# Graph network on one core: the dense pass writes no rows of its second norm, and the second attention's first pass normalises first-norm rows where a flag asks for it

## What is computed

```python
x = _layernorm(x + _L0_gnn_ref(x, src, dst, edge_weight, ...))     # GIN: two linear layers with batch norm
x = _layernorm(x + _L1_gnn_ref(x, edge_index, W, a))               # graph attention over src, 0 for nodes that are no src
x = _layernorm(x + _L2_gnn_ref(x, edge_attr_8, Wq, Wk, Wv, Wo, src, dst))   # attention over dst, 0 for nodes that are no dst
x = _layernorm(x + _L3_gnn_ref(x, edge_index, W, ...))             # graph attention with self loops
```

## Time and profile before

| | |
|---|---|
| median of 3 runs | 4597.76 us (4596.85 to 4601.44) |
| the profiled execution: time, span | 4595.28 us, 4593.2 us |
| busy share of the span | PE 76%, PE weight loads 57%, DVE 72%, ACT 56%, POOL 64% |
| mean granted TensorE clock | 0.853 |
| read from, written to DRAM | 351.68 MB, 389.16 MB |

### The profile page before, as it was taken

How to read it: one execution, slowest core, us unless ns; L and a number is a source line. 1 busy time by engine, 2 the same in 40 slices (tenths; PEclk the granted TensorE clock), 3 DMA queues, 4 the chain that set the end, 5 groups by cost and what they waited for, 6 DMA issues and landing times. The chain is left out here.

```text
span 4593.2 us, 91353 instructions
## 1 busy us (share of the span) xinstructions
PE 3488.3 (76%) x17524; PEld 2616.9 (57%) x17524; DVE 3319.8 (72%) x11837; ACT 2592.9 (56%) x6036; POOL 2942.8 (64%) x2825
## 2 busy tenths in 40 slices
PE   4899934446999997888888878777769958850587
PEld 2799922224888885555555645555558845530365
DVE  7788833334555567999999979888965577740798
ACT  0687712222666666777777748787854436640376
POOL 0366658885333335777777767888877836667476
PEclk9999955556999998998899877778889979985799
DMA  1688823333444447888888843333345537763344
GB/s 43 182 238 237 236 68 79 80 80 88 161 159 162 162 163 231 275 272 273 272 271 272 272 150 92 99 99 101 99 111 128 127 98 211 211 169 82 95 135 117
DMA packets 450182, 734.81 MB, mean 160 GB/s; under 512 B 171319, under 2 KB 284845, under 8 KB 450028
## 3 DMA queue, kind: packets, MB, share of 16 engines
q1 hardware_dynamic: 276204, 571.18, 40.5%
q0 software_dynamic: 173824, 162.17, 14.8%
HBM read 351.68 MB, written 389.16 MB: 161 GB/s over the span
## 5 line engine op out<-in xcount | busy, mean ns | idle before, releaser
L1222 PE MATMUL nodes_xp<-w_self,nodes_x3T 128*125 128x256 f32 x1600 | 493.6, 436 | 130.3 <-DVE nodes_elu L1333 123.5
L1080 POOL TENSOR_TENSOR mlp_r_parts<-mlp_r,mlp_r_parts 128x500 fp32r<-128x500 f32 x200 | 253.5, 1268 | 403.4 <-ACT mlp_r_parts L1066 394.2
L1371 POOL TENSOR_SCALAR nodes_x<-nodes_u,nodes_r,nodes_nm 125x256 f32<-125x256 f32 x800 | 459.8, 588 | 74.6 <-DVE nodes_nm L1326 67.8
L1222 PEld LDWEIGHTS nodes_xp<-w_self,nodes_x3T 128*125 128x125 f32 x1600 | 296.5, 206 | 208.7 <-issue 114.4
L774 PE MATMUL gram<-gin_both,gin_am 125*128 125x257 f32 x404 | 206.6, 667 | 266.2 <-DVE gin_both L757 254.0
L1379 POOL TENSOR_TENSOR nodes_v<-nodes_elu,nodes_x 125x512 f32<-125x512 f32 x200 | 253.7, 1269 | 176.6 <-DVE nodes_elu L1333 176.3
L1105 DVE BATCH_NORM_STATS2 mlp_stats<-mlp_y 128x500 f32 (+1 forms) x200 | 136.2, 681 | 255.6 <-ACT mlp_y L1056 255.6
L774 PEld LDWEIGHTS gram<-gin_both,gin_am 125*128 125x128 f32 x404 | 118.5, 323 | 354.2 <-issue 322.8
L178 POOL DMA_INDIRECT by_src<-rank_recs,rank_place x100 | 119.7, 1197 | 289.9 <-DVE rank_recs L504 289.3
L1019 PE MATMUL mlp_y<-mlp_hT,mlp_w 128*128 128x500 f32 x1200 | 296.7, 396 | 1.6 <-DVE mlp_hT L1099 0.9
L1019 PE MATMUL mlp_y<-mlp_r_parts,mlp_w 128*128 128x500 f32 x1200 | 287.4, 388 | 0.8 <-ACT mlp_y L1056 0.8
(11 more groups left out here) (406 smaller groups left out, 11561.4 us busy)
## 6 DMA issues: line engine op xcount, KB each, us to landing
X<-nodes_x SPq DMA_DIRECT2D x200, 448.0 KB
Y<-mlp_y SPq DMA_DIRECT2D x100, 500.0 KB
nodes_y<-Y SPq DMA_DIRECT2D x100, 500.0 KB
rank_xin<-x SPq DMA_DIRECT2D x100, 448.0 KB
XP<-rank_xc SPq DMA_DIRECT2D x100, 448.0 KB
mlp_h<-XP SPq DMA_DIRECT2D x100, 448.0 KB
nodes_x<-x SPq DMA_DIRECT2D x100, 448.0 KB
out<-nodes_out SPq DMA_DIRECT2D x100, 448.0 KB
```

Of the source, the lines that this page charges most:

```text
L1080: pool.tensor_tensor(rp[:, s, 1, m, :], r[:, s, m, :], rp[:, s, 0, m, :], ALU.subtract).then_inc(s_rp, 1)
L1222: pe.matmul(xp[:, b, j, :], x3T[:, s, k, P * j:P * j + P], w_self[:, k, 0:F], start=(k == 0), stop=False)
L1371: pool.tensor_scalar(dst[:, s, j, :], u[:, at.slot(LONG), j, :], r[:, s, k, j:j + 1], nm[:, s, k, j:j + 1], ALU.mult, ALU.add).then_inc(do ...
```

## The change

- The dense pass computes and stores no x2: two instead of three values of q, r and nm per row, two instead of four POOL instructions per tile at line 1371, no x2 store. SP loads a chunk's x ahead of its y, in place of y ahead of x.
- X1 and X2 become the two halves of one DRAM table XX of 2N rows; Y2 is laid over the second half, which the first attention then fills with the true x2 of every src node, by indices `write2`, computed on POOL ahead of its first gather.
- A dst that is no src has no x2 in the table. To know which, `histogram` adds SHIFT = 16384 to the table of places by dst wherever the count by src of the same node isn't zero. So these edges are scattered to a second region of the sorted list, both regions being cleared by two more DMAs beforehand, and `segments` loads both and adds them up. The fourth number of the record, now 1, comes out as the flag: 1 where the record lay in the second region.
- `attention_scores` gathers a dst row from dst + N * flag (`dst2`), a src row always from src + N. Each `xd` row goes through a layer norm, which for flag 1 has the variance replaced by 1 and the mean by 0. DVE does `stats`, `aggregate`, `variance`, ACT does `normed` (Ln, Exp, Copy, Identity), its result `xn` takes the place of `xd` in the transposes and the D2 store. `xs` gets 8 buffers. The lags and the order of the lists change as shown.

```diff
@@ histogram
+    by_dst = env["sorted"][1]
+    halves = [by_dst[a:a + E, :].rearrange("(p k u) r -> p k (u r)", p=P, k=10) for a in (0, SHIFT)]
...
+            for rows in halves:
+                sp.dma_start(rows, env["zcol"][0:P, 0:120].unsqueeze(1).broadcast_to([P, 10, 120])).then_inc(s_clear, 16)
...
+            ch.step(dve.tensor_scalar(incl[:, 0, :, :], count[:, 0, :, :], 1.0, float(SHIFT), ALU.min, ALU.mult))
+            ch.step(dve.tensor_tensor(base[:, 1, :, :], base[:, 1, :, :], incl[:, 0, :, :], ALU.add))
@@ segments
+            sp.dma_start(far[:, :, :], beyond).then_inc(s_dma, 16)
+            sp.dma_start(nxt_far[0:P - 1, :], beyond[1:P, 0, 0:2]).then_inc(s_dma, 16)
...
+            ch.step(dve.tensor_tensor(env["srec"][1][:, :, :], env["srec"][1][:, :, :], far[:, :, :], ALU.add))
+            ch.step(dve.tensor_tensor(nxt[:, 1, :], nxt[:, 1, :], nxt_far[:, :], ALU.add))
+            ch.step(dve.tensor_copy(env["srec"][1][:, :, 3], far[:, :, 3]))
@@ nodes
-                for k, (m, a) in enumerate(((1.0, EPS), (1.0 + EPS, EPS * EPS), (1.0 + EPS + EPS * EPS, EPS ** 3))):
+                for k, (m, a) in enumerate(((1.0, EPS), (1.0 + EPS + EPS * EPS, EPS ** 3))):
...
-                for k in range(3):
+                for k in range(2):
...
-                for k, (dst, done, stored) in enumerate(((x1, s_x1, o_1), (x2, s_x2, o_2))):
...
+                for j in range(J):
+                    pool.tensor_scalar(x1[:, s, j, :], u[:, at.slot(LONG), j, :], r[:, s, 0, j:j + 1], nm[:, s, 0, j:j + 1],
+                                       ALU.mult, ALU.add).then_inc(s_x1, 1)
@@ attention_scores
-                dram.gather(xd[:, s, :], env["X2"], meta["node"][:, at.col], s_d[s])
-                dram.gather(xs[:, s, :], env["X2"], meta["other"][:, at.col], s_s[s])
+                dram.gather(xd[:, s, :], env["XX"], dst2[:, at.col], s_d[s])
+                dram.gather(xs[:, l, :], env["XX"], src2[:, at.col], s_s[l])
...
+            def normed(at):
+                s = at.slot(RING)
+                act.wait_ge(s_q, at.count(2, 2))
+                ch = Chain(act, ca, at.count(3))
+                ch.step(act.activation(lnq[:, s, :], q[:, s, :], ACT.Ln, bias=rec[:, at.col, 3]))
+                ch.step(act.activation(c[:, s, :], lnq[:, s, :], ACT.Exp, scale=-0.5))
+                ch.step(act.activation(nm[:, s, :], mean[:, s, :], ACT.Copy, scale=c[:, s, :]))
+                wait(act, s_t, at.count(1, 1 - RING))
+                wait(act, s_o[s], at.uses(RING, 32))
+                act.activation(xn[:, s, :], xd[:, s, :], ACT.Identity, bias=nm[:, s, :], scale=c[:, s, :]).then_inc(s_xn[s], 1)
...
-            run_stages(act, [(0, copy_rows), (1, copy_out)], T)
+            run_stages(act, [(0, normed), (1, copy_rows), (3, copy_out)], T, **stages)
...
+            def variance(at):
+                s = at.slot(RING)
+                dve.wait_ge(s_mv, at.count(1, 1))
+                wait(dve, s_xn[s], at.uses(RING))
+                dve.scalar_tensor_tensor(out=q[:, s, :], in0=mv[:, s, 1:2], scalar=EPS, in1=fresh[:, at.col],
+                                         op0=ALU.add, op1=ALU.mult).then_inc(s_q, 1)
+                dve.tensor_scalar(mean[:, s, :], mv[:, s, 0:1], unfresh[:, at.col], None, ALU.mult).then_inc(s_q, 1)
...
-            run_stages(dve, [(0, rest), (1, dots)], T)
+            run_stages(dve, [(0, stats), (3, rest), (0, aggregate), (4, dots), (0, variance)], T, **stages)
```

More of the change, by code:

```diff
@@ L49 @@
 RC = 12
+SHIFT = 1 << 14
 CUTS = ((0, 112), (112, 13))
@@ L1379, in add @@
                 pool.tensor_tensor(v[:, s, :, :], el[:, s, :, :], x3[:, at.slot(LONG), :, :], ALU.add).then_inc(s_v, 1)
-            run_stages(pool, [(11, add), (6, first_two)], tiles, tiles, LONG, LONG)
+            run_stages(pool, [(11, add), (6, first)], tiles, tiles, LONG, LONG)
     ph.end()
@@ L1421, in _ @@
         def _(pool):
-            dram = Rows(ph, pool, N)
+            dram, second = Rows(ph, pool, N), Rows(ph, pool, 2 * N)
+            pool.tensor_scalar(write2[:, :], meta["write"][:, :], N, None, ALU.add).then_inc(s_index, 1)
+            pool.wait_ge(s_index, 1)
             def fetch(at):
@@ L1434, in put_x2 @@
                 pool.wait_ge(s_x2, at.count(1, 1))
-                dram.scatter(env["X2"], meta["write"][:, at.col], x2[:, s, :], s_w2[s])
+                second.scatter(env["XX"], write2[:, at.col], x2[:, s, :], s_w2[s])
             def put_xp(at):
@@ L1843, in attention_scores @@
     meta, rec = env["meta"][1], env["srec"][1]
-    xd, xs = ph.sb("xd", [P, RING, F]), ph.sb("xs", [P, RING, F])
+    LONG = 2 * RING
+    xd, xs, xn = ph.sb("xd", [P, RING, F]), ph.sb("xs", [P, LONG, F]), ph.sb("xn", [P, RING, F])
+    st, mv = ph.sb("stats", [P, RING, 6]), ph.sb("mv", [P, RING, 2])
+    q, mean, lnq, c, nm = (ph.sb(n, [P, RING, 1]) for n in ("q", "mean", "lnq", "c", "nm"))
+    fresh, unfresh = ph.sb("fresh", [P, T]), ph.sb("unfresh", [P, T])
+    dst2, src2 = ph.sb("dst2", [P, T], I32), ph.sb("src2", [P, T], I32)
+    s_index = ph.sem("index")
+    stages = dict(unroll=LONG, behind=LONG)
     xT = ph.sb("xT", [128, RING, 2, 4, P], F32R)
@@ L1902, in project @@
                 mm.then_inc(s_p, 1)
-            run_stages(pe, [(0, turn_rows), (1, project)], T)
+            run_stages(pe, [(0, turn_rows), (1, project)], T, **stages)
         @block.scalar
         def _(act):
+            def normed(at):
[8 more added lines that the diff above has]
+                act.activation(xn[:, s, :], xd[:, s, :], ACT.Identity, bias=nm[:, s, :], scale=c[:, s, :]).then_inc(s_xn[s], 1)
             def copy_rows(at):
```

128 lines of the change are left out of this document (73 added, 55 removed).

## The result

The changed kernel takes 4710.03 us (median of 4 runs, 4705.79 to 4713.15), the kernel before 4598.89 us on the same chip (4 runs, 4596.85 to 4601.44): ratio 1.0244, 95% interval 1.0228 to 1.0261. The prediction was 4695 us in a range of 4655 to 4745, slower. The profiled execution took 4713.15 us with a span of 4710.0 us, 116.8 more than the span before. DVE is busy for 71% of it, PE 74%, ACT 58%, POOL 58%; 352.28 MB were read and 339.16 MB written.

A forecast was written before the change was run, and what follows sets the result against it. DVE was taken to bound the dense pass, and a DVE-ACT loop the second attention's first pass, in place of POOL. -34 + 2 + 101 + 20 + 1 + 0.5 + 1 + 6 = +97.5 us on 4595.3; median 4695, range 4655 to 4745.

The forecast's parts named there:

- The loop over DVE and ACT: Second attention's first pass: DVE and ACT wait for each other every tile, 4.04 us against POOL's 3.03, +101 us.
- The clock: Second attention's first pass: PE at its low clock for a third of the tiles, 4.67 us each, +20 us.
- The dense pass: DVE's list gets 0.35 us shorter per pair of tiles, mostly through fewer POOL instructions: -34 us over 97 pairs.
- the order of loads: Dense pass: SP loading x ahead of y delays the first y once, +2 us.
- The stores: Dense pass: 51.2 MB fewer stores to DRAM delay nobody on DVE's list, so they count nothing.
- the wait inside nm: Dense pass: DVE's first nm instruction still waits for POOL's add, 0.64 us a pair.
- The small terms: Ahead of the dense pass: +1 us for two histogram instructions, +6 us for the loads and add of segments.
- The first attention: POOL computes write2 ahead of its first gather there, +0.5 us; its further work unchanged.
- A clock that stays low: Rival: PE's clock stays low in the second attention's first pass, 4.67 us a tile, about 4738 us; 10%.
- POOL as the bound: Rival: no loop, POOL still bounds the second attention's first pass at 3.03 us a tile, about 4574 us; 6%.
- A dense pass that gives back far more: Rival: POOL's add or the outs slide into gaps left by x2, up to 130 us, about 4599 us; 5%.
- dots without its waits: Rival: DVE's semaphore waits in dots cost nothing, loop at 3.56 us a tile, 4647 us; 2%.

The follow-up runs named there:

- Experiments 1: Changed kernel with DVE running variance ahead of dots in the second attention's first pass: 4611.19 us.
- 2: Changed kernel with ACT's list in the second attention's first pass reordered to copy_out, copy_rows, normed: 4585.51 us.
- 3: Changed kernel with one more small chained ACT instruction, a copy of q into nm, at the head of normed: 4728.32 us.
- 4: Changed kernel with variance put between the second and third instruction of dots on DVE, in the second attention's first pass: 4628.43 us.
- 9 to 11: Changed kernel with the second attention's first pass written out for DVE and ACT (4665.55 us), DVE alone (4679.53) or ACT alone (4694.66).
- experiment 6: Changed kernel with POOL writing a second norm of every row in the dense pass into an unread, unstored buffer: 4737.81 us.
- experiment 7: Kernel of experiment 2 with SP's first chunks of the dense pass loaded y ahead of x: 4583.65 us.
- experiment 5: Changed kernel with the dense pass storing each chunk of x1 a second time, into a table nobody reads: 4711.72 us.
- experiment 8: Kernel of experiment 7 with DVE's nm moved ahead of elu in the dense pass: 4563.45 us.

## Why the prediction was right, and where it was off

**The loop over DVE and ACT** was the right mechanism. Experiments 1 and 2 break it, 3 lengthens it, 4 and 9 to 11 shorten it, and the stage follows each time. Its terms:

| term | predicted | in the hardware loop | written out |
|---|---|---|---|
| dots | 1.53 | 1.65 | 1.30 |
| variance and the hop | 0.32 | 0.48 | 0.32 |
| normed | 1.29 | 1.47 | 1.39 |
| copy_rows | 0.48 | 0.46 | 0.46 |
| qs and the hop | 0.42 | 0.42 | 0.42 |
| sum | 4.04 | 4.48 (mean 4.42) | 3.89 |

(In the loop: the tile from 3450.81; written out: that from 3409.67, whose Ln starts at 3411.29. In the six quicker tiles of a turn normed takes 1.40 in the loop too and the sum is 4.39, so the loop hardly touches that term.) The prediction's terms were a mixture. It took dots from the middle of a stage, inside the hardware loop, and variance and normed from the end of another, where the iterations are written out. So 4.04 lies between the two, and no tile takes it. The rows would have told: the score inside the loop stands in the earlier trace rows as "125x8 f32 x1", in written-out tiles as "125x8 f32<-125x8 f32 x1". Beyond that normed was undersized by 0.10 us, since Ln and `nm` take 0.29 us here, where the Ln of the earlier trace rows took 0.19. From the first `prod` to the last the stage now takes 423.0 us (3386.3 to 3809.3), an average of 4.27 us over 99 periods, where it took 296.9 before: +126 us, for which the sum had 101, 25 too few. The other +6 us are the way to the first `prod`, 21.5 us against 15.6; the sum had 1.

**The clock** was the step that failed: "With a third of the tiles at the low clock", +20 us. The granted clock in the stage is 0.94, although PE is busy for only 297 of 447 us (67%), less than in the first attention, where 75% go with 0.75. To read a clock off the busy shares of other stages was no method. And where the clock does fall, it costs little. In experiment 3 (mean clock 0.88) the granted clock is 0.50, the low level of 1.2 GHz, from 3502.4 to 3504.5, in a project that began behind an idle of 1.85 us, and 1.00 in the next project. (Behind the same idle of 1.85 us in front of the project of 3492.15 it had stayed at 1.00.)

```profile
3501.42 2.30 PE L1924 MATMUL att_kq<-att_w_parts,att_xT 128*125 128x256 f32 x12 [1.85 <-DVE att_xT L1996]
...
3506.04 1.69 PE L1924 MATMUL att_kq<-att_w_parts,att_xT 128*125 128x256 f32 x12 [0.24 <-DVE att_xT L1996]
```

Still its stage is only 22 us longer, which the added link explains alone. The changed kernel shows the same in itself: its project of 3538.16 took 2.84 us in place of 1.69, at a clock of 0.50, and from the `prod` of 3539.15 to the next are 4.55 us, as at that place of every turn. From 3440 to 3790 the clock fell nine times, each time for less than a tile, and PE's idle time in a tile takes that up. So the prediction's price for such a tile, 4.67 in place of the loop's own length, was wrong too. A loop term too small by 25 us and a clock term too large by 20 nearly cancelled. So the number was nearer (4695 against 4710) than its parts.

**The dense pass**: predicted -34 for the pairs and +2 for the order of loads, measured -26.1 (-28.8 from the first add, of which experiment 6 gives 22.8 to POOL's instructions). Right in place and in kind. A pair got 0.30 us shorter on average, where 0.35 had been worked out. Averaged over those pairs between 2000 and 2500 us whose rows are grouped alike (31 before, 32 after), start to next start, the outs behind nm go from 1.08 to 0.83 us, 0.25 where 0.28 had been worked out, and nm from 0.86 to 0.80, where 0.07 had been. From the q to these outs it takes 0.70 us, and took 0.71 with one q more: the wait for ACT grew by what the q freed, as the prediction said. Times 97 pairs 0.30 us are 29, which fits the -28.8. The order of loads put the first add 2.7 us later, where 2 had been worked out, but by experiment 7 the pass as a whole takes as long in either order: with y first the first pairs lose what the first add gains. The stores cost nothing, by experiment 5. That the wait inside nm would stay was right too, and experiment 8 shows that moving nm gets back only 0.21 of its 0.64 us, since the q takes the wait over.

**The small terms**: +6.9 for histogram and segments, against 7. So near a hit is luck: in the other twelve traces, whose code is the same up to there, the mark of 1769.0 stands between 1767.6 and 1774.7. The first instruction behind the loads starts at 611.70, where it was 607.30; it is an add of 1.41 us.

```profile
611.70 1.41 DVE L627 TENSOR_TENSOR srec<-srec,seg_far 125x1200 f32<-125x1200 f32 x1 [16.51 <-DMA seg_next_far<-by_dst]
```

**The first attention** is 5.9 us longer, for which the prediction had 0.5. In the traces of the twelve experiments, whose code there is that of the changed kernel, it takes 655.5 to 661.8 us with a median of 657.7, against 655.2 in the one trace of before. So most of it is scatter between executions; what remains isn't settled.

**The rivals.** A clock that stays low: excluded by 0.94. POOL as the bound: false for this kernel, and true for that of experiment 2, whose 4585.5 us stand near the 4574 worked out for it. A dense pass that gives back far more: no. dots without its waits: not here, but the rival had a true core. Written out, dots takes 1.30 us and not 1.53.

**The range.** Its low end was added up wrongly: a loop of 3.9 us, the high clock and -50 for the dense pass give 4645 with the small terms, not 4655. The measured time lies far from that end.

## What to carry to other kernels

- A stage in which no engine is busy for over 70% can still be full: look for two engines that wait for each other once per tile, and follow both lists. If the path comes back within one iteration, the sum of its links is the period. The cure is the order or the lag of one step (125 us for moving `copy_out`), not less work. Work for an older tile belongs in front of work that waits for another engine's newest result.
- Before you take a duration from a row, ask whether it stands inside the hardware loop or in a written-out iteration, and take all terms of one sum from the same kind. Where a chain of small instructions sets the period, writing it out was worth 12% of it here.
